# ScalarE's copy of the second half's transposes placed ahead of the rounding of attention chunk 1

## The reference, cut to what matters

```python
rkv = inputs @ W_rkv + b_rkv;  r, k, v = split(rkv)
r = sigmoid(r);  k = exp(k);  kv = k * v
u1, u2 = scan(a * state + [kv, k])                    # along the tokens
x_att = (u1 + gamma * kv) / (u2 + gamma * k + 1e-06) * r
x = layernorm(inputs + x_att @ W_o + b_o)
x_prev = x shifted by one token (zeros at the start of a sequence)
xr = mu_r * x + (1 - mu_r) * x_prev                   # xk likewise with mu_k
out = layernorm(x + sigmoid(xr @ W_r.T) * (square(relu(xk @ W_k.T)) @ W_v.T))
```

## Time and profile before

| what | value |
|---|---|
| median of 3 runs | 2763.93 us (2758.83, 2763.93, 2767.05) |
| span of the profiled execution, first to last instruction | 2760.2 us |
| PE busy | 2582.5 us, 94% of the span |
| DVE busy | 2410.0 us, 87% |
| POOL, ACT busy | 1227.9 us and 1112.7 us, 44% and 40% |
| mean granted TensorE clock | 0.980 |
| DMA | 110.94 MB, q1 busy for 11.8% |

### The profile page before, as it was taken

One profiled execution on the slowest core, in us unless ns is written; L12 is line 12 of the kernel. 1 busy time (PEld: TensorE's weight loads), 2 busy tenths in 40 slices (PEclk: granted clock), 3 DMA queues, 4 the chain that ended last, 5 costly groups with the idle time before them and its releaser, 6 DMA issues.

```text
span 2760.2 us, 36072 instructions
## 1 busy us (share of the span) xinstructions
PE 2582.5 (94%) x12800; PEld 2185.4 (79%) x12800; DVE 2410.0 (87%) x3275; ACT 1112.7 (40%) x1935; POOL 1227.9 (44%) x779
## 2 busy tenths in 40 slices
PE   7899999999999999999999999999999999999997
PEld 5678887778887788877888877887788877788886
DVE  8898898888898888998889989889888899898884
ACT  4334343434443343443434443434434343434343
POOL 3444444444443444544444434445344444444453
PEclk9999999999999999999999999999999999999998
DMA  4011011011011110100111101101001111011000
GB/s 164 8 39 47 31 47 35 27 48 47 31 42 36 33 47 31 47 31 32 47 35 42 39 24 46 46 31 47 31 31 46 31 48 39 24 46 47 31 31 24
DMA packets 57806, 110.94 MB, mean 40 GB/s; under 512 B 7040, under 2 KB 7040, under 8 KB 57088
## 3 DMA queue, kind: packets, MB, share of 16 engines
q1 hardware_dynamic: 57600, 108.31, 11.8%
HBM read 74.73 MB, written 33.55 MB: 39 GB/s over the span
## 4 chain that ended last, share of the span: by engine, by line
PE 48%; DVE 24%; issue 16%; POOL 8%; ACT 2%; DMA 1%; SPq 0%; DVEq 0%; POOLq 0%; ACTq 0%
PE bankB L792 7%; PE bankB L790 7%; PE bankB L791 7%; PE bankA L773 5%; PE bankA L774 5%; PE bankA L775 5%; PE bankB L838 5%; PE bankB L840 4%; PE bankB L839 4%; DVE xk_f L662 3%; DVE att_f L616 3%; POOL rstd L317 3%; POOL att_f L308 3%; DVE key L601 3%; DVE xr_f L662 3%
## 5 line engine op out<-in xcount | busy, mean ns | idle before, releaser
L773 PE MATMUL bankA<-x_hi,wrkv_hi 128*128 128x512 f32 x1536 | 611.0, 398 | 81.5 <-DVE kv L595 58.4
L774 PE MATMUL bankA<-x_lo,wrkv_hi 128*128 128x512 f32 x1536 | 603.4, 393 | 0.0
L775 PE MATMUL bankA<-x_hi,wrkv_lo 128*128 128x512 f32 x1536 | 602.6, 392 | 0.0
L308 POOL TENSOR_TENSOR att_f<-att_f,gate 128x512 f32<-128x512 f32 x128 | 204.7, 1599 | 594.3 <-DVE att_f L621 594.3
L608 DVE RECIPROCAL gate<-gate 128x512 f32<-128x512 f32 x128 | 429.2, 3353 | 4.4
L773 PEld LDWEIGHTS bankA<-x_hi,wrkv_hi 128*128 128x128 f32 x1536 | 291.4, 190 | 154.9 <-DVE kv L595 71.9
L838 PE MATMUL bankB<-xk_hi,wk_hi 128*128 128x256 f32 x1024 | 305.7, 298 | 69.4 <-ACT zT L438 67.4
L775 PEld LDWEIGHTS bankA<-x_hi,wrkv_lo 128*128 128x128 f32 x1536 | 291.2, 190 | 62.2
L774 PEld LDWEIGHTS bankA<-x_lo,wrkv_hi 128*128 128x128 f32 x1536 | 291.7, 190 | 56.4
L417 ACT ACTIVATE key<-bankA,b_sb 128x512 f32<-128x512 f32 x128 | 86.6, 676 | 562.6 <-PE bankA L775 550.3
L330 POOL TENSOR_TENSOR t<-t,y 128x512 f32<-128x512 f32 x128 | 191.5, 1517 | 257.2 <-DVE t L682 257.2
(11 more groups left out here) (84 smaller groups left out, 6020.0 us busy)
## 6 DMA issues: line engine op xcount, KB each, us to landing
x_f<-in_xT SPq DMA_DIRECT2D x128, 256.0 KB, 3.9
y<-in_x SPq DMA_DIRECT2D x128, 256.0 KB, 2.7
out<-t SPq DMA_DIRECT2D x128, 256.0 KB, 2.0
wrkv_f<-in_w_rkv SPq DMA_DIRECT2D x3, 768.0 KB, 6.8
wo_f<-in_w_o SPq DMA_DIRECT2D x1, 1024.0 KB, 10.2
wr_f<-in_w_r SPq DMA_DIRECT2D x1, 1024.0 KB, 12.0
wk_f<-in_w_k SPq DMA_DIRECT2D x1, 1024.0 KB, 13.9
wv_f<-in_w_v SPq DMA_DIRECT2D x1, 1024.0 KB, 15.8
```

The source lines that it names most:

```text
L308: pool.tensor_tensor(att_f[:, c], att_f[:, c], gate[:, c % 2], ALU.mult).then_inc(att_made, 1)
L773: pe.matmul(bank[:], w_hi, x_hi[:, h], start=(h == 0), stop=False)
L774: pe.matmul(bank[:], w_hi, x_lo[:, h], start=False, stop=False)
L775: last = pe.matmul(bank[:], w_lo, x_hi[:, h], start=False, stop=(h == NC - 1))
```

## The change

In ScalarE's `step` the two ACTIVATEs of `copy_zT(s1, 1)` stand ahead of the one of `att_high(s, 1)` and no longer behind it. It concerns the 31 steps in which s1 exists. No instruction is added or taken away, no wait changes, and the orders of PE, DVE, POOL and SP are the same. The tail (`last_block`) is not touched.

```diff
                 exp_key(s, 2)
                 exp_gate(s, 2)
+                if s1.exists():
+                    copy_zT(s1, 1)
                 att_high(s, 1)
                 if first:
                     weight_high(W_K)
                 if s1.exists():
-                    copy_zT(s1, 1)
                     tanh(s1, 0)
                     key_square(s1, 0)
                     previous_scaled(s1, 1, s)
```

## The result

| kernel | median | runs | span of the profile | mean granted clock |
|---|---|---|---|---|
| before | 2762.02 us | 4 | 2760.2 us | 0.980 |
| changed | 2789.56 us (2787.66 to 2800.99) | 4 | 2785.8 us | 0.978 |

The ratio is 1.010, with a 95% interval of 1.0076 to 1.0123: the change costs 1.0%, 27.5 us. Forecast were 2756 us, in a range of 2722 to 2842 that holds the time, and faster as the likeliest sign, which is wrong. One execution of each kernel was profiled; that of the changed kernel was its fastest.

The account below looks back on a forecast made before the run. TensorE's wait for zT's copy bounds it, DVE right behind. Gains of 22 us (inner steps) and 17 (loop turns) less 23 (clock) make 16; 8 lost where POOL is first: 2763.9 - 16 + 8 = 2756 us, range 2722 to 2842.

Parts of the forecast that it names:

- What bounds the kernel: TensorE's wait for zT before the keys of half 0, 67.4 us in 30 steps; DVE a second bound right behind.
- TensorE's side: Keys of half 0 done 3.95 us earlier, 2.46 where the clock had not fallen; xr_lo from 1063.19 instead of 1067.14.
- DVE's walk: L601 just ahead of xr_lo, L605 blocked behind it; V of s2 starts 1.5 us earlier, after a 2.4 us wait.
- The clock: Falls after V's new wait in two thirds of 23 steps, 1.5 us each: 23 us lost, bounds 0 and 35.
- the close place: L601 against xr_lo, 0.18 us apart; POOL first in half of six steps after loop turns, 8 us lost.
- the likeliest case: The forecast of 2756 us, chance 0.42: L601 ahead of xr_lo in most steps, L605 blocked.
- my own sum: A step with POOL first ends 2.3 us later and has its clock fall for certain, 2.8 us in all.
- the turns of the loop: Six steps where V of s2 started 1.7 to 5.0 us later than elsewhere after the change: 17 us gained.
- Rival 3: POOL ahead of L601 in most steps: 71 us lost, 2835 us; 2775 to 2820 if in part; chance 0.33.
- rivals 2 and 3: Rival 2: clock does not fall at V's new wait, 2733 us, chance 0.06; Rival 3: 2835 us, chance 0.33.
- the forecast case: L601 ahead of xr_lo in most steps, L605 blocked: 2756 us, own range 2740 to 2770, chance 0.42.

Follow-up runs that it names:

- e5: The changed kernel, with POOL waiting for u2_saved of chunk 3 (the copy just before L601) before xr_lo of half 1; 2758.72 us, ratio 0.9972.
- e4: The changed kernel with one more VectorE instruction, a copy of one column, before L601 of chunk 3; 2810.16 us, ratio 1.0148.
- e6: e3 with a second wait of POOL, for den_made of chunk 1 before xr_lo of half 0; 2618.75 us, ratio 0.9469.
- e7: The kernel before (copy behind the rounding) with both POOL waits of e6; 2685.50 us, ratio 0.9712.
- e1: The changed kernel, with POOL waiting for scale_made of chunk 3 (end of L605) before xr_lo of half 1; 2716.15 us, ratio 0.983.
- e3: The changed kernel, with POOL waiting for den_made of chunk 3 (end of L601) before xr_lo of half 1; 2707.52 us, ratio 0.9798.
- e2: The kernel before with the same POOL wait as e1; 2763.95 us, ratio 0.9995.

## Why the prediction was wrong

*What bounds the kernel:* right. The keys' wait for zT went entirely, the keys of half 0 run at full clock, and DVE's `key_low` is the second bound, reached at once.

*TensorE's side:* right. In the step at 1045.56 `xr_lo` comes 22.08 us after the first R product, where 1063.19 - 1041.11 = 22.08 was worked out.

*DVE's walk:* right to 0.1 us in the step for which it was made. L601 was laid at 21.90 us after R and came at 21.83 in that step; L605 blocked at 2.77 us; V of s2 at 46.84 us with a wait of 2.19, for 46.74 and 2.4. In a step with POOL first, V came at 49.32, for 1090.2 - 1041.1 = 49.1. How the ordinary steps differ from this one was not seen (below). L605's blocking, which the Trainium skill's rule gave ("SBUF — State Buffer", "Who interferes with whom") and no row of before showed, is shown now in all 27 steps of e5 in which it meets POOL, at 2.77 to 2.79 us. The other half of the rule was put too widely in the prediction. The Trainium skill exempts an instruction with one SBUF input only outside the modes that use two ports, and the trace does not agree with an exemption of all: in the kernel before, a copy of four columns with one input started inside a POOL instruction (1032.96 to 1035.60) and stood still until its end:

```profile
1033.22 2.40 DVE L668 COPY zT<-zT 128x4 f32<-128x4 f32 x1
```

The reciprocals keep their 3.35 us in all runs; in which mode the copy ran no run shows.

*The clock:* right in the number: two thirds of the steps with the new wait were forecast, 14 of 21 measured. That it would fall "for certain" in a step with POOL first was wrong: 7 of 10.

**The step that failed is the close place: the number of steps in which POOL comes first, put at half of six, and with it the choice of the likeliest case.** The runs show 14 in its place: all six behind a turn of the loop, and eight more. I gave L601 0.05 to 0.2 us of lead in most steps and took that for a won race outside the six. The lead was 0.24 us in seven steps, 0.01 to 0.07 in fifteen, and in five, all behind a turn of the loop, L601 came 0.03 to 0.10 us too late. The seven are the steps whose new block begins a sequence, and the step that I walked through is one of them. An ordinary step has two things more on DVE ahead of L601, which the trace of before showed and the prediction names nowhere: a copy of four columns in place of a memset, 0.07 us, and a scan that starts from the carry, 1.27 us for 1.21. In the step at 1128.74:

```profile
1148.77 0.16 DVE L669 COPY zT<-zT 128x4 f32<-128x4 f32 x1
1148.84 1.27 DVE L591 TENSOR_TENSOR_SCAN u<-lam,carry,key 128x512 f32<-128x512 f32 x1
```

Besides, numerator 2 comes 0.14 us later after R there than in the step at 1045.56 (L622 at 12.85 and 12.71 us), where 0.08 had been taken from the rows of before. With 0.04 us less for the mixes that is 0.23 us, and `xr_lo` stays at 22.07 after R: L601 comes at 22.06 in place of 21.83. And the race is not won by any lead: L601 lost with up to 0.04 us of it and won from 0.04 on.

So 14 steps turned where I had counted three. With 11 more at the 2.8 us of my own sum that is 31 us on 2756, 2787; measured 2789.6. The price itself was right: 87.0 us for a turned inner step against 84.3. e5, in which no step turns, lies at 2758.7, beside the forecast; the 17 us of the sum for the turns of the loop stand in its profile (499.3 us for these six steps, 516.3 before). Rival 3 named the mechanism, its price and the point at which it turns, and 2775 to 2820 "if only part of the steps turn" got a chance of 0.06; it was the case that an edge narrower than the error of the sum makes the likeliest. Where the steps are spread over both sides of an edge, the mixture has to carry the chance, not the two pure cases. That the range holds the time is owed to rivals 2 and 3, over which it reaches, and not to the forecast case.

*Not foreseen:* the keys of half 1 wait 1.3 us for DVE's `gated_values` in the turned steps. By the sum it costs nothing of its own, being part of the same lateness that V would have waited for (1.29 + 3.29 = 4.6 us, 4.8 worked out). The tie of the scan with `xk_lo` at half 0 was in the trace of before (lost in one step) and is not in the sum. It costs the changed kernel nothing that can be seen: the steps with a lost scan and the ones behind them take 169.2 and 167.6 us in pairs, two steps of the first kind 168.5, because L601 and `xr_lo` don't meet in the second of the pair.

*What stays open:* what decides a tie within 0.04 us. The runs show who won, with the start times of the trace, and no more; at half 0 the scan won and lost with the same 0.02 us of lead. How far the number of turned steps differs between executions is open too, since each kernel has one profile; the four runs of the changed kernel lie 13 us apart.

## What to carry to other kernels

Before taking a wait off the bounding engine, ask which two chains now move against each other, and list the instructions of DVE and POOL that stand a few tenths of a microsecond apart on them, in an ordinary step and in each special one: the gain of the moved copy went into two blocked instructions of another engine. Where two such instructions meet, put the order in by hand with a wait of the one that has slack, for the semaphore of the one that has none. If a race is closer than the error of the estimate, forecast the mixture.

## What the hardware showed that I had not expected

- 0.07 us of extra work in a step was enough that L601 came first in no step but the seven with 0.24 us of lead (e4), where it had come first in six more. Two waits of POOL, two lines of code, brought 5.3% together with the copy's move (e6).
- A four-column copy, 0.16 us alone, takes 2.4 us when it comes after the start of a POOL instruction (2.37 us in the changed kernel, 0.16 in e6); where it is free, in e6 and e7, the wait for kv is gone.
- POOL starts 0.07 to 0.09 us after the end of the DVE instruction that it waits for (e1 and e3; in e3 L603 ends at 1044.92 and `xr_lo` starts at 1045.00), while DVE's own next instruction starts 0.03 us after it. A semaphore between engines is thus enough to lose a race to one's own producer, and e3 was built on the opposite.
- A longer wait at one place need not cost its length: e2 has five more lost scans than the kernel before, with 2.1 us more wait for kv each, and the same time.
